# A causal attention and mixture-of-experts layer on one core: the value product in three pieces, and VectorE's batch work in another order

## The reference, cut to what matters

```python
y = einsum('bnd,hde->bhne', layernorm(x), Wkqv) + bkqv      # k 128, q 128, v 8 per head
A = einsum('bhnd,bhmd->bhnm', q, k) / sqrt(128)
A = softmax(where(tril, A, -inf))
sa = einsum('bhnm,bhmd->bnhd', A, v).reshape(8, 512, 128)
x = x + sa @ Wp + bp
h = layernorm(x)
shared = down(silu(gate(h)) * up(h))
scores, idx = top_k(sigmoid(h @ router_w.T + routing_bias), 2)
x = x + shared + sum over the two experts of score * expert(h)
```

## Time and profile before

| | us |
|---|---|
| three timed runs | 731.1, 731.4, 735.19 |
| median of them | 731.4 |
| span of the profiled execution | 730.7 |
| TensorE busy in the span | 654.0 |
| VectorE busy | 541.8 |
| ScalarE busy | 456.8 |
| GpSimd busy | 310.2 |

### The profile page before, as it was taken

The page is one execution under the profiler, slowest core; times in us unless marked ns, Lnnn a source line. Parts: engine busy times, 40 slices in busy tenths (PEclk is TensorE's granted clock), DMA queues, the critical chain, the costliest instruction groups (busy, mean ns, idle before and its releaser), DMA issues.

```text
span 730.7 us, 16418 instructions
## 1 busy us (share of the span) xinstructions
PE 654.0 (90%) x5432; PEld 398.4 (55%) x5432; DVE 541.8 (74%) x1903; ACT 456.8 (63%) x816; POOL 310.2 (42%) x512
## 2 busy tenths in 40 slices
PE   7488999999999999998899999999986779899992
PEld 6264455545554554554445455455565568777652
DVE  6699877787788778788877877868546655567796
ACT  3376676767667776765676776666762545565651
POOL 4493531314123223221477522313465356565773
PEclk9699999999999999999999999999998889999997
DMA  9100443621122101221132111021444257695424
GB/s 255 53 2 20 133 128 105 175 77 45 49 74 44 32 32 42 77 70 37 49 93 85 45 51 42 17 44 64 102 107 107 73 117 145 126 164 120 110 60 126
DMA packets 102768, 60.24 MB, mean 82 GB/s; under 512 B 44568, under 2 KB 94640, under 8 KB 102688
## 3 DMA queue, kind: packets, MB, share of 16 engines
q1 hardware_dynamic: 66144, 28.22, 16.2%
q10 hardware_dynamic: 32336, 22.29, 10.4%
q0 software_dynamic: 4208, 8.69, 4.6%
HBM read 19.62 MB, written 30.77 MB: 69 GB/s over the span
## 4 chain that ended last, share of the span: by engine, by line
PE 63%; DVE 17%; ACT 6%; issue 6%; another core or an unknown queue 2%; POOL 1%; ACTq 0%; DVEq 0%; POOLq 0%
PE bank L1019 8%; PE bank L1040 7%; PE bank L1056 7%; PE bank L1042 6%; PE bank L1041 6%; DVE junk L1427 5%; PE bank L1136 4%; PE bank L1138 4%; PE bank L1137 4%; PE bank L982 3%; PE bank L984 3%; PE bank L983 3%; DVE ql L1399 3%; ACT p_sb L1299 2%
## 5 line engine op out<-in xcount | busy, mean ns | idle before, releaser
L1299 ACT ACTIVATE p_sb<-bank,inv_scale 128x512 f32<-128x512 f32 (+1 forms) x384 | 222.0, 614 | 40.6 <-PE bank L1042 33.3
L1427 DVE CUSTOM_DVE_ANT_0 junk<-bank,causal 128x512 bf16<-128x512 f32 (+3 forms) x512 | 221.8, 483 | 31.4 <-PE bank L1019 29.0
L914 POOL TENSOR_SCALAR_AFFINE_SELECT p_sb<-p_sb 128x384 f32<-128x384 f32 x128 | 67.0, 524 | 306.5 <-ACT p_sb L1299 305.9
L1041 PE MATMUL bank<-ql,ah 128*128 128x512 f16 (+3 forms) x512 | 153.4, 300 | 0.0
L1042 PE MATMUL bank<-qh,al 128*128 128x512 f16 (+3 forms) x512 | 153.0, 300 | 0.0
L1019 PE MATMUL bank<-ah,qh 128*128 128x512 f16 (+3 forms) x512 | 132.5, 303 | 21.8 <-DVE low L1427 20.3
L1040 PE MATMUL bank<-qh,ah 128*128 128x512 f16 (+3 forms) x512 | 147.2, 300 | 0.8 <-ACT p_sb L1299 0.8
L1399 DVE TENSOR_TENSOR ql<-bank,qh 128x512 f16<-128x512 f32 x128 | 88.5, 691 | 64.7 <-ACT qh L1264 61.3
L1264 ACT ACTIVATE qh<-bank 128x512 f16<-128x512 f32 x128 | 76.5, 597 | 62.4 <-PE bank L984 60.3
L1611 DVE SCALAR_TENSOR_TENSOR al<-bank,gu_scale,ah 128x512 f32<-128x512 f32 x69 | 51.6, 748 | 61.3 <-ACT ah L1330 41.9
L1019 PEld LDWEIGHTS bank<-ah,qh 128*128 128x128 f16 x512 | 50.1, 98 | 79.7 <-DVE low L1427 47.6
(11 more groups left out here) (247 smaller groups left out, 1130.2 us busy)
## 6 DMA issues: line engine op xcount, KB each, us to landing
o_dram<-oT ACTq DMA_DIRECT2D x32, 256.0 KB, 2.3
ys_dram<-ql ACTq DMA_DIRECT2D x25, 256.0 KB
xs_dram<-causal ACTq DMA_DIRECT2D x6, 832.0 KB, 4.8
wst<-in_Wkqv SPq DMA_DIRECT2D x8, 264.0 KB, 5.0
x_sb<-in_x SPq DMA_DIRECT2D x8, 256.0 KB, 5.8
out<-x_sb SPq DMA_DIRECT2D x8, 256.0 KB
o_all<-o_dram SPq DMA_DIRECT2D x7, 256.0 KB
r_all<-r_dram SPq DMA_DIRECT2D x7, 256.0 KB
```

The source lines that it names most:

```text
L1041: nc.tensor.matmul(bank, m.ah[:, keys], ql[:, s, c * P:N], start=False, stop=False)
L1299: nc.scalar.activation(p_sb[v % P_RING][:, S_AT[k]:S_AT[k] + S_WIDTH[k]], m.psum[S_BANK[k]][:, 0:S_WIDTH[k]], ACT.Exp, scale=m.inv_scale[: ...
L1427: last = nc.vector.tensor_tensor_reduce(out=junk[:, (3 * u + k) % 2, at:at + w], in0=m.psum[M_BANK[(3 * u + k) % 2]][:, at:at + w], in1=m. ...
```

## The change

The value product of groups 0 to 30 is cut into three pieces, one in each of three successive slots: key chunk 0 in slot 15 + 4g (t mod 4 = 3), chunk 1 in the next (t mod 4 = 0), chunks 2 and 3 in the one after (t mod 4 = 1). The last group stays whole. ScalarE's copy to `oT` moves to the end of the slot of the last piece, behind the exponentials, and its transfer is issued right after it. VectorE does its batch work (`scale_weights`, `after_attention`, `send_rows` and a new `place_rows` that was the end of `send_rows`) ahead of `ql` in every slot of the attention. The batch steps get other offsets: `rinv` 3, `mult` 5, `proj` 6, statistics 7, aggregate and Newton 8 and 9, `norm` 9; `split` and `logits` stay at 10 and 14. SyncE issues the transposed maxima's store ahead of the gather, and the spreading of the inverses behind the second move. The conversion of the expert weights starts one slot later, its low halves one per slot.

```diff
--- before.py
+++ after.py
@@ -445,30 +445,37 @@
 LAG = 10
 LOW_AT = GROUP + 2
 PV_AT = GROUP - 1 + LAG + 2
+PV_PIECES = ((0,), (1,), (2, 3))
+PV_LAST = len(PV_PIECES) - 1
 FFN_AT = UNITS + LAG
 
 SORTS = 7
 PLACE_LATE = -(-(PV_AT - LOW_AT) // GROUP)
-STEPS = {"rinv": 0, "mult": 2, "proj": 4, "stats": 6, "aggr": 6, "newton0": 6, "newton1": 7, "newton2": 7, "norm": 8, "split": 10, "logits": 14}
+STEPS = {"rinv": 3, "mult": 5, "proj": 6, "stats": 7, "aggr": 8, "newton0": 8, "newton1": 9, "newton2": 9, "norm": 9, "split": 10, "logits": 14}
 LATE_LOGITS = 16
 NEVER = 10 ** 6
 LAST_STEPS = {"gather": 1, "rinv": 2, "spread": 3, "mult": NEVER, "proj": 4, "stats": 4, "aggr": 4, "newton0": 5, "newton1": 5, "newton2": 5, "norm": 5, "late": 6, "late_copy": 7, "logits": 8, "exp": 9, "split": 10}
-PART_STEPS = {"sort": 18, "weigh": 22, "count": 23, "rank": 26, "place": 26, "expert": 30, "send": 27}
-LAST_PART_STEPS = {"sort": 9, "weigh": 10, "count": 11, "rank": 12, "place": 12, "expert": 13, "send": 13}
-SORT_LATE = ((0, 0, 0, 1, 2, 3, 4), (0, 0, 0, 0, 1, 1, 1))
+PART_STEPS = {"sort": 15, "weigh": 24, "count": 23, "rank": 26, "slots": 27, "place": 28, "expert": 30, "send": 28}
+LAST_PART_STEPS = {"sort": 9, "weigh": 10, "count": 11, "rank": 12, "slots": 12, "place": 12, "expert": 13, "send": 13}
+SORT_LATE = ((0, 1, 3, 4, 5, 5, 7), (0, 0, 0, 0, 1, 1, 1))
+
+
+def first_step(b):
+
+    return PV_AT + H - GROUP + 2 + H * b
 
 
 def step_at(name, b):
 
     if (name, b) == ("logits", B - 2):
-        return step_at("rinv", b) - STEPS["rinv"] + LATE_LOGITS
-    return PV_AT + H - GROUP + 2 + H * b + (STEPS if b < B - 1 else LAST_STEPS)[name]
+        return first_step(b) + LATE_LOGITS
+    return first_step(b) + (STEPS if b < B - 1 else LAST_STEPS)[name]
 
 
 def part_step_at(name, g):
 
     b = SPLITS[g][1] // TB - 1
-    return step_at("rinv", b) - (STEPS if b < B - 1 else LAST_STEPS)["rinv"] + (PART_STEPS if b < B - 1 else LAST_PART_STEPS)[name]
+    return first_step(b) + (PART_STEPS if b < B - 1 else LAST_PART_STEPS)[name]
 
 
 def sort_at(k, g):
@@ -500,13 +507,26 @@
 
     g, r = divmod(t - at, GROUP)
     return g if r == 0 and 0 <= g < GROUPS else None
+
+
+def pieces_at(t):
+
+    if t == PV_AT + GROUP * (GROUPS - 1):
+        return GROUPS - 1, tuple(range(TB))
+    g, r = divmod(t - PV_AT, GROUP)
+    return (g, PV_PIECES[r]) if 0 <= g < GROUPS - 1 and r < len(PV_PIECES) else None
+
+
+def weighed_at(t):
+
+    return GROUPS - 1 if t == PV_AT + GROUP * (GROUPS - 1) else next((g for g in range(GROUPS - 1) if t == PV_AT + GROUP * g + PV_LAST), None)
 
 
 W_MAX_AT, W_MAX_EVERY = 11, GROUP
 W_SQ_AT = W_MAX_AT + W_MAX_EVERY * E + 1
 W_SUM_AT = W_SQ_AT + 4
 W_SHARED_AT = W_SUM_AT + 8
-W_SPLIT_AT, W_SPLITS = W_SHARED_AT + KINDS + 2, 2
+W_SPLIT_AT, W_SPLITS = W_SHARED_AT + KINDS + 3, 2
 
 
 def w_split_at(i):
@@ -516,7 +536,7 @@
 
 def w_low_at(i):
 
-    return W_SPLIT_AT + GROUP * (i // W_SPLITS) + W_SPLITS
+    return W_SPLIT_AT + GROUP * (i // W_SPLITS) + W_SPLITS + i % W_SPLITS
 
 
 ZERO_AT, ZERO_EVERY, ZERO_TILES = 12, 3, 13
@@ -847,17 +867,19 @@
                     if step_at("split", b) < LOW_AT + GROUP * g <= step_at("split", b) + GROUP:
                         store_rows(b)
                         turn_rows(b)
-                if g >= PLACE_LATE and (g - PLACE_LATE) % PER_BATCH == PER_BATCH - 1:
-                    gather_products((g - PLACE_LATE) // PER_BATCH)
-                    spread_inverses((g - PLACE_LATE) // PER_BATCH)
                 sp.wait_ge(t_taken, T_TURN["low", g] + 1)
                 sp.dma_start(m.c_dram[g * GROUP * TB:(g + 1) * GROUP * TB, :], lowT[g % 2][:, :]).then_inc(low_stored, 16)
+                gathered = (g - PLACE_LATE) // PER_BATCH if g >= PLACE_LATE and (g - PLACE_LATE) % PER_BATCH == PER_BATCH - 1 else None
+                if gathered is not None:
+                    gather_products(gathered)
                 sp.wait_ge(low_stored, 16 * (g + 1))
                 if g >= 1:
                     sp.wait_ge(low_placed, 16 * g)
                 at = g * GROUP % RING
                 sp.dma_start(qh[0:1, at:at + GROUP, :].rearrange("p u n -> p (u n)"),
                              m.c_dram[g * GROUP * TB:(g + 1) * GROUP * TB, :].rearrange("(o r) n -> o (r n)", o=1)).then_inc(low_placed, 16)
+                if gathered is not None:
+                    spread_inverses(gathered)
             sp.wait_ge(low_placed, 16 * GROUPS)
             sp.wait_ge(q_done, UNITS)
             for quad in quads:
@@ -1042,20 +1064,21 @@
                     last = nc.tensor.matmul(bank, m.al[:, keys], qh[:, s, c * P:N], start=False, stop=True)
                 last.then_inc(s_done, 1)
 
-            def weigh_values(g):
-                pe.wait_ge(p_masked, 2 * GROUP * (g + 1))
-
-                if g >= 1:
-                    pe.wait_ge(oT_ready, g)
-                else:
-                    pe.wait_ge(o_clear, 1)
-                for c in range(TB):
+            def weigh_values(g, pieces):
+                if pieces[0] == 0:
+                    pe.wait_ge(p_masked, 2 * GROUP * (g + 1))
+                    if g >= 1:
+                        pe.wait_ge(oT_ready, g)
+                    else:
+                        pe.wait_ge(o_clear, 1)
+                for c in pieces:
                     w = N - c * P
                     for j in range(GROUP):
                         v = g * GROUP + j
                         last = nc.tensor.matmul(m.psum[O_BANK][32 * j:32 * j + V1, c * P:N], m.v_sb[:, v // H * TB + c, v % H, :], p_sb[v % P_RING][:, P_AT[c]:P_AT[c] + w],
                                                 start=(c == 0), stop=(c == TB - 1), skip_group_check=True)
-                last.then_inc(pv_done, 1)
+                if pieces[-1] == TB - 1:
+                    last.then_inc(pv_done, 1)
 
             def turn(name, n):
                 if T_TURN[name, n] > 0:
@@ -1221,8 +1244,8 @@
                     turn_shared(k)
                 if t < FFN_AT:
                     after_attention(t)
-                if (g := group_at(t, PV_AT)) is not None:
-                    weigh_values(g)
+                if pieces_at(t):
+                    weigh_values(*pieces_at(t))
                 for k in range(3):
                     if 0 <= t - LAG < UNITS:
                         score(t - LAG, k)
@@ -1281,12 +1304,6 @@
                     nc.scalar.activation(m.shared_raw[:, k * 512:min(EW, k * 512 + 512)], bank_t[:, 0:min(512, EW - k * 512)], ACT.Copy).then_inc(t_taken, 1)
                 if t < FFN_AT:
                     split_rows(t)
-                if (g := group_at(t, PV_AT)) is not None:
-                    act.wait_ge(pv_done, g + 1)
-
-                    if g >= 2:
-                        act.wait_ge(o_stored[g % 2], 16 * (g // 2))
-                    nc.scalar.activation(oT[g % 2][:, :], m.psum[O_BANK][:, :], ACT.Copy).then_inc(oT_ready, 1)
                 v = t - LAG
                 for k in range(3):
                     if 0 <= v < UNITS:
@@ -1298,7 +1315,11 @@
                             act.wait_ge(scale_chain, 2)
                         nc.scalar.activation(p_sb[v % P_RING][:, S_AT[k]:S_AT[k] + S_WIDTH[k]], m.psum[S_BANK[k]][:, 0:S_WIDTH[k]], ACT.Exp,
                                              scale=m.inv_scale[:, v % H:v % H + 1]).then_inc(exp_done, 1)
-                if (g := group_at(t, PV_AT)) is not None:
+                if (g := weighed_at(t)) is not None:
+                    act.wait_ge(pv_done, g + 1)
+                    if g >= 2:
+                        act.wait_ge(o_stored[g % 2], 16 * (g // 2))
+                    nc.scalar.activation(oT[g % 2][:, :], m.psum[O_BANK][:, :], ACT.Copy).then_inc(oT_ready, 1)
                     act.wait_ge(oT_ready, g + 1)
                     act.dma_start(m.o_dram[g * P:(g + 1) * P, :], oT[g % 2][:, :]).then_inc(o_stored[g % 2], 16)
                 i, r = divmod(t - ZERO_AT, ZERO_EVERY)
@@ -1547,7 +1568,7 @@
                     for k in range(2):
                         last = nc.vector.tensor_tensor(weight[:, k, at], top[:, 2 * k, at], top[:, 3, at], ALU.mult)
                     c.link(last)
-                if (g := part_at("rank", t)) is not None:
+                if (g := part_at("slots", t)) is not None:
                     dve.wait_ge(t_taken, T_TURN["rank", g] + 1)
                     counts_at = len(CHUNKS[g]) * P
                     c.link(nc.vector.tensor_tensor(above[:, :, :], ranks[:, counts_at:counts_at + E].unsqueeze(2).to_broadcast([P, E, FULL]),
@@ -1560,6 +1581,9 @@
                         last = nc.vector.tensor_tensor(slot_of[:, at:at + T, :], ranks[:, i * P:i * P + T * E].rearrange("p (t e) -> p t e", e=E),
                                                        first_slot[:, g, :].unsqueeze(1).to_broadcast([P, T, E]), ALU.add)
                     c.link(last)
+
+            def place_rows(t):
+                c = sort
                 if (g := part_at("place", t)) is not None:
```

(20 more changed lines are left out.)

## The result

The changed kernel takes 790.66 us (median of 4; the kernel before beside it 732.56). The ratio is 1.078, with a 95% interval from 1.074 to 1.081: slower by 58 us where 40 were forecast, and above the range (746 to 784). The profiled execution took 788.45 us, its span is 786.7; one run of the four at a lower clock is left out of the ratio.

What follows compares the result with a forecast made beforehand. TensorE, busy 654.0 of 730.7 us, takes turns as the limit with the latency of the chain from projection to M2. The terms sum to +40.4 on 730.7, so 771, median 772; range 746 to 784.

Steps and rivals of the forecast that it cites:

- change 1: Value product in three pieces: two more crossings in each of 31 groups, +12.4 us; two plain slots lose their wait, -6.2.
- change 2: Late copy to `oT` and its transfer delay `qh` in the low slot, 3.81 instead of 3.14 us, 28 times: +18.8.
- The zero fills: Line 1307's transfers on ScalarE fall behind the copy in slots 21 and 33 instead of 15 and 27: +0.6 us.
- changes 3 and 4: GpSimd steps one slot ahead of their readers, six batches: `mult` before `proj` +7.7 us, `norm` before `split` +12.4.
- The 0.7 for the lost slack of `proj`: Projection of each batch no longer sits partly in a chain's slack: 0.7 us more.
- Rival A: GpSimd isn't late, so `mult` and `norm` one slot ahead cost nothing but 0.7 us: 747 us; chance 0.13.
- Rival B: Copy and transfer don't hold up `qh`, minus 19.4, but GpSimd waits grow, plus 8: 760 us; chance 0.13.
- Rival C: Neither `qh` nor GpSimd is late and VectorE's work hides wholly: 721 us, chance 0.06; half-hidden form 728, chance 0.06.
- change 5: VectorE's batch work ahead of `ql` hides most of 16.9 us of stalls, 6.4 kept: -10.5 us.
- Weights and queues: Moved weight conversions fit free time on ScalarE and VectorE, and SyncE's new order delays nothing needed: 0 us.
- The end of the attention: Slot 127 to first gate activation: +5.7 us, including batch 6's waits for `mult`, +3.1, and `norm`, +1.4.

Runs made afterwards that it cites:

- e6: The kernel before with the value product's last chunk moved behind the first scores of the same slot, adding one crossing; ratio 1.0100.
- e1: The changed kernel with the copy to `oT` ahead of the exponentials again, its transfer still behind them; 780.61 us, ratio 1.061.
- e2: The changed kernel with `mult` and the steps from aggregate to `norm` one slot earlier; 762.91 us, ratio 1.033.
- e3: The changed kernel with unused products added to keep TensorE busy in its waits for `proj` and `split`; 783.78 us, ratio 1.067.
- e10: e7 with the value product whole again, keeping the new order and slots of VectorE's batch work; ratio 1.0071.
- e7: e4 with the conversion of the expert weights back in its old slots; ratio 1.0049.
- e12: The kernel before, unchanged, run again for its trace; the kernel before takes 732.96 us in that set.
- e4: The changed kernel with the copy ahead of the exponentials and `mult` and aggregate to `norm` one slot earlier; 740.61 us, ratio 1.009.

## Why the prediction was wrong

**The pieces and crossings (change 1): right.** Slots of 3.90, 3.69 and 3.69 to the hundredth; e6 gives 0.22 for a crossing.

**The copy (change 2): right** in its mechanism and size; e1 takes it away and the low slots are 3.14. The zero fills issued in slots 21 and 33 were put at 0.49 each. Slot 34 is 0.53 longer than the 3.81 forecast for its kind, but slot 22 is 1.80 longer. Most of that is of this one execution: in e2 and e3, with the same order, slot 22 takes 4.34 and 4.35.

**`mult` and `norm` (changes 3 and 4): right, slightly small.** The six projection slots exceed 3.90 by 2.3 to 2.5 (slot 67 without its clock stretch), of which 0.89 is TensorE's own work, as in e2; that leaves 9.0 us of waits for 7.7 forecast. The six split slots exceed it by 1.95 to 2.41, 13.7 for 12.4. (The 7.65 at which the prediction has `norm` ready is 0.04 more than its own 4.48 and 3.13; that changes nothing here.) The 0.7 for the lost slack of `proj` is right too: TensorE's own work for `proj` and `logits` is 7.1 us, 0.9 above the prediction's 6.2 for the kernel before. Rival A is excluded: e2 removes both waits. Rival B, a copy that holds up nothing, is excluded by e1, where low slots fall from 3.84 to 3.14. Rival C needed both, so it falls as well.

**VectorE's work (change 5): the sum was nearly right, the reason is only half shown.** In the other slots 7.1 us stand above their kinds (37, 53, 58, 69, 85, 101, 117 and smaller ones), and the low slots ahead of the splits are shorter by 2.1; that leaves 5.0 where 6.4 were forecast. e10 shows the condition for slots 36 and 37 only: the same work costs more over a base of 2.95.

**"Weights and queues ... Nothing for both": failed.** SyncE's loads wait for low halves that come two slots later; slot 75 costs 1.2. e7 shows the cause. I looked for work in the slots the weights moved to, and didn't ask what queues behind the load that waits for them.

**The failed step is the sum itself: it priced every new wait by its length and had no term for what TensorE does after it.** Behind four of the twelve waits for GpSimd's steps in the attention (1.2 to 2.2 us long) the granted clock fell to 1.2 GHz, for 3.4 us at a time, at 1.6 us each. That is 6.3 us, shown by e3, which keeps the waits and loses these stretches. The trace of the kernel before had such a stretch, at 339.6, in a slot where VectorE's batch work held TensorE, and I took the 1.6 as part of a stall. Which of the waits are followed by a stretch no run explains (e12 has the same stand without one), so from that trace the term could have been named and priced, but not counted.

**The end of the attention: mis-sized.** `proj` of batch 6 stands 3.82 (3.5 forecast), and ScalarE's split 3.99, 1.7 more than before (1.4 forecast): that is right. But 12.2 us were added and not 5.7, and 10.2 us of this stretch (from 562.5 and from 579.6) run at half the clock, none before. e3, which fills these waits too, has 39.9 us there instead of 44.2, so 4.3 of the 6.5 us are the clock's. Another 0.85 is a copy that the sum left out: it charged the copy to 28 low slots, but the last one stands in slot 137, ahead of the first gate activation. From that slot's first scores to that activation it is 4.73 us in e2 and e3, which copy late, and 3.88 in e1 and e4, which copy early. The last 1.35 I can't put down to one step.

Together: 6.3 (clock) + 1.2 (slot 75) + 1.3 (zero fills) + 2.6 (waits) make 11.4, where the attention has 11.0 beyond its forecast (smaller differences nearly cancel); the end adds 6.5; the start gives 0.7 back and the network 1.2. The clock alone, 6.3 and 4.3, is 10.6 of the 15.6 us between the forecast span of 771.1 and the measured 786.7. The terms that were read slot by slot held; the range left no room for a cost that comes behind a wait.

## What to carry to other kernels

Where a change makes TensorE stand for a microsecond or two once a batch, look at the granted clock of the stretch behind such a stand in the trace you already have, and give it a term of its own. A cut that ends a product later moves everything that hangs on its end; give the whole chain its distance, down to the last consumer, before you judge the cut: e4 has the same pieces and is 0.9% slower than the kernel before, not 7.8%. And for each transfer ask what stands behind it in its queue, not only when its own data are wanted.

## What the runs showed of the hardware

- A stand of 2.10 us of TensorE was followed by 3.4 us at 1.2 GHz, with back-to-back work in it, slots 3.69 to 5.28 (180.2, and alike at 316.7 and 453.3); products that nobody uses, put into the same wait, left the clock at 1.00. Not each wait does it: of two waits of 1.24 the one in slot 35 was followed by none and the one in slot 67 by one; those of 2.13 and 2.10 in slots 87 and 119 by none; and the stand of 2.5 us in slot 83 of the kernel before by one in its first trace and by none in e12.
- The issue of a transfer on ScalarE right behind another took 1.72 us once (slot 22), and slot 22 was 1.3 us shorter with the same order in e3.
- The slots of the attention without batch work are the same on both chips (3.90, 3.69, 3.69 and 3.14 in e4 and e7), while first to last gate activation take 180 to 186 us on the first and 150 to 152 on the second, for every kernel. The kernel before takes 732.96 to 734.52 on the first and 701.49 on the second. In the windows above the second chip's DMA queues are 0.98 busy at 180 GB/s and TensorE hardly waits; the first's are 0.64 busy at 141 GB/s. Which transfer is slower on the first wasn't looked into.
